# Gathers of a deformable convolution: how many leave at a time, and how far ahead of the matmuls

## The chip, the cores and the metric

The kernel runs on one core of one Trainium2 chip. The metric is device time of one execution in microseconds (us), the median of several runs. TensorE is called PE here, VectorE DVE, ScalarE ACT, GpSimd POOL and SyncE SP, as in the profile.

## The reference

The input x is 4 images of 64 channels and 32 x 32 pixels. Two layers follow each other, both with a residual:

```python
x = x + conv_ref(_ln_c(x), offset_w, offset_b, mask_w, mask_b, weight, bn...)
#   offset = conv3x3(x) + offset_b; mask = sigmoid(conv3x3(x))
#   for each pixel and each of 9 taps: 4 corners around a shifted position,
#   gathered from x, weighed bilinearly, times mask; einsum with weight; batch norm; silu
t = _to_tokens(x)
t = t + ffn_ref(_ln_t(t), sigma, phi, M_u, M_phi_plus, M_phi_minus, log_weights, gumbel)
#   causal convolution of all channels with 16 filters phi (and with alternating signs),
#   mixed by the matrices M_phi (weights of 4 branches of different length), plus 3 lags by M_u
```

## The kernel before

The pixels of two images (a pair, `bp` = 0 or 1) are processed together. A pair has 4 *quarters* of 256 tokens, so there are 8 quarters `q`. A quarter has 4 blocks `k` (2 pixel parities p x 2 images b2), each of 128 pixels x 9 taps. For each block and tap POOL issues one indirect DMA (`G<-corner_table,idx`, line 296): it fetches 128 rows of 1 KB, the four corners, from a table in DRAM, by the indices `idx`. That is 36 gathers a quarter, 288 in all, in the order of blocks and taps; `i` = 9k + tap counts them in their quarter. `G` has one slot for each block, so the gathers of a block also wait until the block of the quarter before has been weighed (`v_ready`).

DVE weighs a block when its nine gathers have landed (`weigh`, lines 490 to 494: three TENSOR_TENSOR, the last writes `V`). PE transposes V (`turn_values`, lines 905 and 906), ACT copies it to vT (line 696), PE convolves it with the weights (`convolve_values`, line 915), ACT copies y_chan (line 701), PE turns it back (`turn_convolved`, line 921), ACT takes the exponential (line 706, `expo`), and DVE does silu, residual and the second layer norm (`finish` = `activate` + `normalise`, lines 502 to 525), which ends with `u_ready`. `positions(q)` and `weights(q)` on DVE make the indices and corner weights of a quarter two ahead.

The second layer is 8 *passes* `n`, one per quarter. A pass has 16 steps (`convolve(i)`, lines 1017 to 1028: f16 matmuls into two PSUM banks by turns, 3(j+1) matmuls a step, j = n mod 4, so passes 3 and 7 are the longest and 0 and 4 the shortest). After each step ACT copies the bank to `u_conv` (line 739), and a later step waits for that copy. `conv_done[b2]` counts the steps: step i raises `conv_done[i % 2]`. Every fourth step PE mixes a group (`mix_group`, line 978), which ends with `group_mixed`; ACT's copy of `mixed` (line 744) waits for that after the last group of a pass. `HOSTED_AT` puts the PE work of the first layer for quarter n + 1 into pass n: `turn_values` at steps 5 and 12, `convolve_values` at 6 and 13, `turn_convolved` at 7 and 14. Between two passes lies a chain: exponential, `finish(q, 1)`, then the matmuls of `step_odd_tokens` (line 992).

Ahead of pass 0 stands the prologue: layer norm, the convolution for offsets and masks of both pairs (`convolve_offsets`, line 852, then `turn_offsets`, 862), normalised pixels turned (`turn_normalised`, 833; counted by `n_turned`), mixing matrices summed (882, `mats_summed`), filter rows made and stored (`f_rows_ready`), the second pair's pixels scaled on ACT (line 640, `n_ready`), the main weights turned (`w_turned`), the whole first layer for quarter 0 (`finish(0, 0)`, `finish(0, 1)`), then four scalings of the mixing matrices and two weighings of quarter 1 on DVE. The gathers of quarter 0 and most of quarter 1 lie in it.

All gathers leave in the order of one instruction stream. `keep_pace(q, i)`, called ahead of each gather, puts waits into POOL's stream that hold gather i of quarter q, and all behind it, until other engines have reached some point. In the passes the point is a step: it is linear in i, STEPS = 16 steps of convolution for BLK x TAPS = 36 gathers, `LEAD` gathers back.

Of the kernel before, what the change touches and what calls it, by code (L numbers as in the profile page):

```python
# [11 lines left out]
BP = B // 2  # L12
# [3 lines left out]
BLK = 4  # L16
TAPS = 9
# [9 lines left out]
STEPS = 4 * N_GROUPS  # L27
HALF = T // 2
BRANCHES = 4
# [3 lines left out]
START = 2  # L33
# [4 lines left out]
RSQRT_SEED = float(0x5F3759DF)  # L38
TAP_HALVES = (range(0, 5), range(5, 9))
WARM_UP = 4  # L40
LEAD = 22
WARM_AGAIN = 6


# [5 lines left out]
def metaformer_kernel(nc, x, offset_w, offset_b, mask_w, mask_b, weight, gamma, beta, mean, var,  # L50
                      sigma, phi, m_u, m_plus, m_minus, log_weights, gumbel, ident_in, grid_in, first_row_in, out):
    ctx = ExitStack()
    with ctx:
# [9 lines left out]
        def ap(a, offset, dims):  # L63
# [104 lines left out]
        x_turned, x_copied, n_ready, n_turned, n_copied = (  # L168
            sem(n) for n in ("x_turned", "x_copied", "n_ready", "n_turned", "n_copied"))
        woff_ready, woff_turned, woff_copied = sem("woff_ready"), sem("woff_turned"), sem("woff_copied")  # L170
        w_ready, w_turned, w_copied = sem("w_ready"), sem("w_turned"), sem("w_copied")
        phi_turned, f_rows_ready, f_rows_stored = sem("phi_turned"), sem("f_rows_ready"), sem("f_rows_stored")
        diag_ready, f_scale_ready, f_scale_done = sem("diag_ready"), sem("f_scale_ready"), sem("f_scale_done")
        w_diag_ready, mats_summed, mu_summed = sem("w_diag_ready"), sem("mats_summed"), sem("mu_summed")
        mats_ready, mu_ready, uT_zeroed = sem("mats_ready"), sem("mu_ready"), sem("uT_zeroed")
        off_done, off_laid, off_turned, off_copied, mask_exp = (
            sem(n) for n in ("off_done", "off_laid", "off_turned", "off_copied", "mask_exp"))
# [3 lines left out]
        v_ready = [sem(f"v_ready{i}") for i in range(2)]  # L181
        val_copied, y_done, y_exp, y_used, u_ready = (
            sem(n) for n in ("val_copied", "y_done", "y_exp", "y_used", "u_ready"))
        val_turned, y_convolved, y_copied = sem("val_turned"), sem("y_convolved"), sem("y_copied")
        u_turned, u_copied = sem("u_turned"), sem("u_copied")
        filt_loaded = [sem(f"filt_loaded{k}") for k in range(K)]
        conv_done = [sem(f"conv_done{i}") for i in range(2)]
# [75 lines left out]
        def _(pool):  # L263
# [4 lines left out]

            def keep_pace(q, i):

                step, last = (STEPS * (q - 1) + STEPS * (m - LEAD) // (BLK * TAPS) for m in (i, i - 1))
                if q >= 2 and (step != last or i == 0):
                    pool.wait_ge(conv_done[step % 2], step // 2 + 1)
                if q == 0 and i == TAPS:
                    pool.wait_ge(off_turned, 2)
                if q == 0 and i in (20, 25, 30):
                    pool.wait_ge(mats_summed, (i - 15) // 5 * 2 + 2)
                if q == 1 and i == 4:
                    pool.wait_ge(n_turned, 8)
                if q == 1 and i == 20:  # L280
                    pool.wait_ge(off_turned, 2 * BP)

            for bp in range(BP):
                for q in range(4 * bp, 4 * bp + 4):
# [838 lines left out]
```

## Time and profile before

| | us |
|---|---|
| median of 3 runs | 618.11 (615.82 to 621.09) |
| the profiled execution | 615.08 |
| its span, first to last instruction | 613.2 |
| PE busy | 466.6 (76% of the span), mean granted clock 0.852 |
| DVE busy | 308.9 (50%) |
| POOL busy | 291.0 (47%) |
| ACT busy | 226.2 (37%) |
| DMA moved | 53.95 MB, 88 GB/s on the mean |

The times in the rows are us from the start of the span unless marked ns. `x20` is a number of instructions put together in one row; the bracket at a row's end is how long the engine had been idle before it and what ended the idleness. "issue" there means that nothing the profile shows was waited for, "remote" that the releaser is unknown. The end of a PE instruction is modelled, not seen; the start of an ACT, DVE or POOL instruction is seen. The granted clock is a share of TensorE's full speed; its levels are 0.5 (1.2 GHz) and 1 (2.4 GHz).

### The profile page before, as it was taken

To read this page: it belongs to the slowest core of one execution; us is meant where nothing else is said; L and a number is where in the kernel's file an instruction comes from. 1 tells how busy PE (TensorE), PEld (TensorE's weight loads), DVE (VectorE), ACT (ScalarE), POOL (GpSimd) and SP (SyncE) were. 2 spreads that over 40 slices of the span, in tenths; PEclk is the share of its full clock that TensorE was granted. 3 is DMA by queue.
4 is the path that set the end of the run, shared out by engine and by line. 5 is a ranking of instruction groups with operands and counts; after the bars stand their busy time and mean duration, and the time that the engine had idled before them with its cause. 6 is when DMAs were issued, how large, how long until landed. Compare 5 with 4: busy or idle time off the path is not lost.

```text
span 613.2 us, 8001 instructions
## 1 busy us (share of the span) xinstructions
PE 466.6 (76%) x3022; PEld 256.5 (42%) x3022; DVE 308.9 (50%) x762; ACT 226.2 (37%) x515; POOL 291.0 (47%) x295
## 2 busy tenths in 40 slices
PE   4967559645666787699879996676678758998996
PEld 3522331422453444345435553444244424554543
DVE  5638752229996365637463746383636363612000
ACT  1126430015433453343434334433344334443432
POOL 1057747470374666466646664755476637000000
PEclk9877767558777898799989998877688969999999
DMA  7925933390132332233313321322133212100000
GB/s 156 177 78 166 339 103 103 96 342 18 36 91 64 87 90 83 64 92 94 86 55 95 87 85 55 100 78 77 56 92 95 86 48 92 33 1 1 10 0 10
DMA packets 43631, 53.95 MB, mean 88 GB/s; under 512 B 24536, under 2 KB 34014, under 8 KB 43593
## 3 DMA queue, kind: packets, MB, share of 16 engines
q0 software_dynamic: 13824, 37.77, 20.7%
q1 hardware_dynamic: 23745, 13.42, 8.5%
q10 hardware_dynamic: 6024, 2.26, 1.7%
q8 instruction: 24, 0.39, 0.3%
q14 instruction: 14, 0.11, 0.1%
HBM read 50.12 MB, written 3.30 MB: 87 GB/s over the span
## 4 chain that ended last, share of the span: by engine, by line
PE 49%; DVE 15%; issue 12%; another core or an unknown queue 10%; ACT 10%; DMA 2%; POOL 1%; SPq 1%; ACTq 0%; DVEq 0%
PE bank L1017 20%; PE bank L978 7%; ACT u_conv L739 6%; PE bank L852 5%; PE bank L1026 3%; PE bank L915 3%; PE bank L833 2%; PE bank L905 2%; DVE G L490 2%; DVE sil L503 2%; PE bank L882 1%; PE bank L862 1%; DMA filt<-in_L_ffn_phi_dram 1%; PE bank L824 1%
## 5 line engine op out<-in xcount | busy, mean ns | idle before, releaser
L296 POOL DMA_INDIRECT G<-corner_table,idx x288 | 288.4, 1001 | 231.4 <-issue 75.3
L1017 PE MATMUL bank<-filt,u 128*128 128x512 f16 (+1 forms) x960 | 206.9, 364 | 3.1 <-ACT u_conv L739 3.0
L739 ACT COPY u_conv<-bank 64x512 f32<-64x512 f32 x256 | 148.5, 580 | 160.4 <-PE bank L1017 60.7
L1017 PEld LDWEIGHTS bank<-filt,u 128*128 128x128 f16 x960 | 93.8, 102 | 104.4 <-issue 29.5
L490 DVE TENSOR_TENSOR G<-G,bank 128x2304 f32<-128x2304 f32 x32 | 81.6, 2551 | 73.2 <-DMA G<-corner_table,idx 71.4
L978 PE MATMUL bank<-u_conv,mixw 128*64 128x256 f32 (+1 forms) x640 | 71.1, 357 | 9.1 <-issue 8.8
L978 PEld LDWEIGHTS bank<-u_conv,mixw 128*64 128x64 f32 x640 | 43.1, 144 | 31.2 <-issue 21.4
L1026 PE MATMUL bank<-filt,u 64*128 64x256 f16 x168 | 30.0, 287 | 29.3 <-ACT u_conv L739 29.1
L494 DVE TENSOR_TENSOR V<-G 128x576 f32<-128x576 f32 x32 | 24.3, 758 | 41.3 <-PE bank L906 27.6
L491 DVE TENSOR_TENSOR G<-G 128x1152 f32<-128x1152 f32 x32 | 43.4, 1358 | 1.1
L502 DVE TENSOR_SCALAR expo<-expo 128x128 f32<-128x128 f32 x16 | 4.0, 250 | 70.1 <-ACT expo L706 51.8
L915 PE MATMUL bank<-vT,w_main 128*64 128x128 f32 (+1 forms) x320 | 27.7, 313 | 10.2 <-issue 6.8
L852 PE MATMUL bank<-filt,w_off 64*32 64x512 f32 x144 | 31.0, 688 | 4.3 <-issue 4.1
L905 PE MATMUL bank<-ident_swap,V 128*128 128x128 f32 x128 | 23.4, 320 | 10.6 <-DVE V L494 5.6
L1026 PEld LDWEIGHTS bank<-filt,u 64*128 64x128 f16 x168 | 11.9, 96 | 44.7 <-ACT u_conv L739 32.0
L1028 PE MATMUL bank<-filt,u_early 64*128 64x256 f16 x168 | 30.0, 287 | 0.0
L696 ACT COPY vT<-bank 128x512 f32<-128x512 f32 x32 | 17.2, 589 | 31.7 <-remote 16.2
L915 PEld LDWEIGHTS bank<-vT,w_main 128*64 128x64 f32 (+1 forms) x320 | 22.3, 158 | 15.0 <-issue 14.9
L905 PEld LDWEIGHTS bank<-ident_swap,V 128*128 128x128 f32 x128 | 18.0, 166 | 13.4 <-issue 13.1
L385 DVE TENSOR_TENSOR offs<-grid,bank 128x216 f32<-128x216 f32 x4 | 1.5, 380 | 34.5 <-PE bank L862 34.5
L761 ACT CAST u<-bank 128x256 f16<-128x256 f32 x8 | 3.0, 372 | 41.6 <-PE bank L994 33.6
L992 PE MATMUL bank<-u,ladder 128*128 128x256 f16 x8 | 2.7, 335 | 19.8 <-DVE u L525 19.8
(174 smaller groups left out, 425.6 us busy)
## 6 DMA issues: line engine op xcount, KB each, us to landing
filt<-filter_rows SPq DMA_DIRECT2D x16, 514.0 KB
G<-corner_table,idx POOLq DMA_INDIRECT x288
corner_table<-n_uT SPq DMA_DIRECT2D x12, 128.0 KB, 3.5
mixw<-in_x_dram SPq DMA_DIRECT2D x2, 512.0 KB, 6.2
filt<-in_L_ffn_M_phi_plus_dram SPq DMA_DIRECT2D x4, 256.0 KB
out_dram<-o_sb ACTq DMA_DIRECT2D x8, 128.0 KB, 2.2
filt<-n_L_ffn_M_phi_minus_dram ACTq DMA_DIRECT2D x2, 256.0 KB
corner_table<-n_uT ACTq DMA_DIRECT2D x4, 128.0 KB, 4.4
```

The lines of the kernel that those rows point to most:

```text
L296: pool.indirect_dma_start(G[:, k, tap, :], None, corners[bp], bass.IndirectOffsetOnAxis(ap=idx[:, q % 2, k, tap:tap + 1], axis=0)).then_in ...
L490: link(dve.tensor_tensor(g, g, w, ALU.mult))
L491: link(dve.tensor_tensor(G[:, k, :, 0:2 * C], G[:, k, :, 0:2 * C], G[:, k, :, 2 * C:4 * C], ALU.add))
L494: dve.tensor_tensor(V[:, b2].rearrange("s (t c) -> s t c", c=C), G[:, k, :, 0:C], G[:, k, :, C:2 * C], ALU.add).then_inc(v_ready[b2], 1)
L739: act.copy(u_conv[C * par:C * par + C, g % 2, :, b2, p, :], conv_ps[b2][rows].rearrange("c (k a) -> c k a", k=GROUP)).then_inc(conv_copied ...
L852: last = pe.matmul(bank[b2][group:group + NCH, :], w_off[half, tap, :], a, start=(t == 0), stop=(tap == TAP_HALVES[tg][-1]))
L905: pe.transpose(val_ps[b2][:, P * m:P * m + P], V[:, b2, P * m:P * m + P], ident)
L915: last = pe.matmul(y_chan_ps[C * b2:C * b2 + C, :], w_main[0:rows, m, :], vT[0:rows, b2, m, :], start=(m == 0), stop=(m == 4))
L978: last = pe.matmul(acc_ps[n % 2][C * p:C * p + C, 0:2 * P].rearrange("e (b a) -> e b a", b=2)[:, :, a0:a1], mixw[:, s, C * k:C * k + C], u ...
L1017: last = pe.matmul(out_of[b2][:, :, a0:P], u16[:, NJ * bp + j2, hl, b2, par:par + 2].rearrange("s w c -> s (w c)"), filt_h[:, ks, par, par ...
L1026: last = pe.matmul(out_of[0][:, :, 0:C], u16[C:P, n, hl, 0, par:par + 2].rearrange("s w c -> s (w c)"), filt_h[C:P, ks, par, part, 2:2 + C ...
L1028: pe.matmul(out_of[1][:, :, 0:C], u_early[:, hl, par:par + 2].rearrange("s w c -> s (w c)"), filt_h[0:C, ks, par, part, 2 + C:2 + P], star ...
```

## The change

Only the waits in POOL's stream change. In the passes (quarters 2 to 7) a wait stands before gathers 0 and 18 alone, and the step that it asks for is counted with LEAD = 14: step 9 of pass q-2 for gather 0, step 1 of pass q-1 for gather 18. Before, nearly every second or third gather had a wait, from step 6 of pass q-2 for gather 0 to step 5 of pass q-1 for gather 35. In quarters 0 and 1, before, six waits stood; after, quarter 0 has 11 and quarter 1 has 13, about one for every three gathers.

```diff
-LEAD = 22
+LEAD = 14
...
             def keep_pace(q, i):
 
-                step, last = (STEPS * (q - 1) + STEPS * (m - LEAD) // (BLK * TAPS) for m in (i, i - 1))
-                if q >= 2 and (step != last or i == 0):
+                step = STEPS * (q - 1) + STEPS * (i - LEAD) // (BLK * TAPS)
+                if q >= 2 and i % (2 * TAPS) == 0:
                     pool.wait_ge(conv_done[step % 2], step // 2 + 1)
-                if q == 0 and i == TAPS:
-                    pool.wait_ge(off_turned, 2)
-                if q == 0 and i in (20, 25, 30):
-                    pool.wait_ge(mats_summed, (i - 15) // 5 * 2 + 2)
-                if q == 1 and i == 4:
-                    pool.wait_ge(n_turned, 8)
-                if q == 1 and i == 20:
-                    pool.wait_ge(off_turned, 2 * BP)
+                if q == 0:
+                    if i == 3:
+                        pool.wait_ge(n_turned, 4)
+                    if i == 9:
+                        pool.wait_ge(off_turned, 2)
+                    if i == 11:
+                        pool.wait_ge(x_turned, 4)
+                    if i == 14:
+                        pool.wait_ge(mats_summed, 2)
+                    if i == 17:
+                        pool.wait_ge(f_rows_ready, 1)
+                    if i == 20:
+                        pool.wait_ge(v_ready[0], START + 1)
+                    if i == 23:
+                        pool.wait_ge(pixels_scaled, 1)
+                    if i == 26:
+                        pool.wait_ge(mats_summed, 2 * BRANCHES - 1)
+                    if i == 28:
+                        pool.wait_ge(v_ready[1], START + 1)
+                    if i == 30:
+                        pool.wait_ge(n_ready, 3)
+                    if i == 33:
+                        pool.wait_ge(w_turned, 1)
+                if q == 1:
+                    if i == 0:
+                        pool.wait_ge(n_turned, 8)
+                    if i == 3:
+                        pool.wait_ge(y_convolved, 1)
+                    if i == 7:
+                        pool.wait_ge(off_done, 3)
+                    if i == 10:
+                        pool.wait_ge(off_done, 4)
+                    if i == 13:
+                        pool.wait_ge(off_turned, 2 * BP)
+                    if i == 15:
+                        pool.wait_ge(v_ready[1], START + 2)
+                    if i == 17:
+                        pool.wait_ge(val_turned, START + 2)
+                    if i == 20:
+                        pool.wait_ge(y_convolved, 2)
+                    if i == 23:
+                        pool.wait_ge(u_ready, 2)
+                    if i >= 27 and i % 3 == 0:
+                        pool.wait_ge(conv_done[1], (i - 24) // 6 + 1)
```

## Rows read from the trace of the kernel before

**Rows 1.** The page's group of the gathers: busy us, mean ns of one, idle.
```profile
L296 POOL DMA_INDIRECT G<-corner_table,idx x288 | 288.4, 1001 | 231.4 <-issue 75.3
```

**Rows 2.** Stretches: length, busy (x) of PE, PEld, DVE, ACT, POOL, clock, DMA.
```profile
198.00:258.00 60.00, 44.81 (x315) 25.41 (x314) 33.64 (x78) 24.62 (x51) 36.12 (x36) 0.87 0.28 82
258.00:318.00 60.00, 52.04 (x347) 27.48 (x346) 33.10 (x78) 24.47 (x50) 35.28 (x36) 0.96 0.28 82
318.00:379.00 61.00, 56.71 (x382) 30.19 (x381) 33.20 (x78) 24.29 (x50) 36.59 (x36) 0.98 0.28 80
379.00:442.00 63.00, 42.09 (x309) 25.20 (x308) 33.48 (x78) 24.39 (x50) 35.81 (x36) 0.74 0.26 78
442.00:503.00 61.00, 43.08 (x313) 24.18 (x312) 30.07 (x61) 24.11 (x49) 37.38 (x36) 0.86 0.27 81
503.00:557.00 54.00, 48.72 (x346) 26.61 (x345) 24.31 (x57) 24.07 (x49) 13.80 (x14) 0.98 0.12 37
557.00:613.00 56.00, 51.57 (x336) 25.91 (x334) 0.00 (x0) 20.85 (x40) 0.00 (x0) 1.00 0.02 6
```

**Rows 3.** ACT's waits from 143 to 526 us: total, times, longest.
```profile
ACT u_conv L739 <- remote: 46.2, 14, 7.5
```

**Rows 4.** Timeline of PE in pass 1 (start, length, what, how many).
```profile
203.01 1.97 PE L978 MATMUL bank<-u_conv,mixw 128*64 128x128 f32 x32
```

**Rows 5.** Timeline of ACT in pass 1.
```profile
201.25 1.19 ACT L739 COPY u_conv<-bank 64x512 f32<-64x512 f32 x2 [1.23 <-PE bank L1017]
...
209.05 0.37 ACT L744 COPY mixed<-bank 128x256 f32<-128x256 f32 x1 [4.77 <-remote]
```

**Rows 6.** Timeline of POOL in pass 1, after its pause.
```profile
209.37 0.95 POOL L296 DMA_INDIRECT G<-corner_table,idx  x1 [1.63 <-remote]
```

**Rows 7.** Busy time by stretch, in the two longest runs with PE at work.
```profile
88.00:98.00 10.00, 9.20 (x61) 2.09 (x58) 6.92 (x16) 1.79 (x6) 7.68 (x8) 0.98 0.36 106
98.00:114.00 16.00, 12.16 (x17) 1.42 (x15) 0.00 (x0) 0.59 (x1) 10.42 (x11) 0.52 0.33 98
383.00:392.00 9.00, 7.38 (x70) 4.77 (x67) 3.91 (x2) 4.45 (x9) 6.86 (x8) 0.87 0.37 106
392.00:402.00 10.00, 4.79 (x27) 2.28 (x22) 2.76 (x2) 2.49 (x5) 6.77 (x7) 0.68 0.34 102
```

**Rows 8.** Timeline of POOL: one of the prologue, first and last of sixteen.
```profile
45.58 0.94 POOL L296 DMA_INDIRECT G<-corner_table,idx  x1 [4.51 <-DVE idx L406]
...
379.22 0.95 POOL L296 DMA_INDIRECT G<-corner_table,idx  x1 [3.87 <-PE bank L1017]
...
399.65 0.95 POOL L296 DMA_INDIRECT G<-corner_table,idx  x1 [0.30 <-issue]
```

**Rows 9.** Timeline of PE in the prologue.
```profile
31.25 5.06 PE L852 MATMUL bank<-filt,w_off 64*32 64x512 f32 x36
...
68.66 0.42 PE L906 MATMUL bank<-ident_swap,V 128*64 128x128 f32 x1
...
88.97 7.66 PE L852 MATMUL bank<-filt,w_off 64*32 64x512 f32 x53
...
113.19 1.01 PE L852 MATMUL bank<-filt,w_off 64*32 64x512 f32 x1 [1.08 <-issue]
...
124.63 2.40 PE L915 MATMUL bank<-vT,w_main 128*64 128x128 f32 x20 [1.51 <-ACT vT L697]
```

**Rows 10.** Timeline of ACT in the prologue, three copies of what PE made.
```profile
84.09 1.07 ACT L696 COPY vT<-bank 128x512 f32<-128x512 f32 x2 [12.12 <-remote]
...
106.85 0.59 ACT L665 COPY filt<-bank 128x512 f32<-128x512 f32 x1 [16.63 <-remote]
...
133.75 0.27 ACT L701 COPY y_chan<-bank 128x128 f32<-128x128 f32 x1 [9.27 <-remote]
```

**Rows 11.** Timeline of DVE in pass 1, a weighing and the end of the pass.
```profile
219.80 2.56 DVE L490 TENSOR_TENSOR G<-G,bank 128x2304 f32<-128x2304 f32 x1 [3.89 <-DMA G<-corner_table,idx]
...
249.81 0.23 DVE L502 TENSOR_SCALAR expo<-expo 128x128 f32<-128x128 f32 x1 [7.25 <-ACT expo L706]
```

## The prediction

> **What bounds the kernel now.** The page comes first: of its span of 613.2 us POOL is busy for less than half, and the gathers, which the change moves, are 288 instructions of POOL of 1.0 us each [rows 1]. The profiled execution took 615.08 us, 1.9 more than its span and 3.0 (0.5%) under the median of 618.11. The sum below is made against 615.1 and is not corrected for that half per cent.
>
> The busy time by stage comes next. The last stretch, 557 to 613 us, has the longest convolutions and no gather, and PE is idle there for 56.0 - 51.6 = 4.4 us; I take that as what a pass loses without gathers. Stretches with 36 gathers leave PE idle for 60 - 44.8 = 15.2, 60 - 52.0 = 8.0, 61 - 56.7 = 4.3, 63 - 42.1 = 20.9 and 61 - 43.1 = 17.9 us, and 503 to 557 for 5.3 [rows 2]. So PE sets the time of the passes, and something tied to the gathers takes PE time from the light ones. Those five and the sixth exceed 4.4 us by 10.8, 3.6, 0, 16.5, 13.5 and 0.9: 45.3 us. For pass 0 I add 3.7, as much as pass 2, and take 49 us.
>
> What takes it? ACT's waits name it badly: "remote", 46.2 us in 14 waits before the copies to u_conv [rows 3]. One of them can be followed. PE's mixing group starts at 203.01 and lasts 1.97 us [rows 4]. ACT, which needs only that for its copy of mixed, starts it at 209.05, 4.1 us after the recorded end, idle for 4.77 us [rows 5]. POOL had paused for a step of PE too, for 1.63 us, and went on at 209.37 [rows 6]. So PE's completions reached nobody for 4 us while a run of gathers drained. In a run a gather takes 0.95 us and the next starts 0.30 behind it [rows 8]. When a run goes on, PE itself starves: from 88 to 98 us PE starts 61 matmuls, from 98 to 114, under one run of gathers (8 and 11 of them in the two stretches), 17 matmuls in 16 us. In the passes the only long run, 16 gathers from 379.2 to 400.6 [rows 8], shows the same: 70 matmuls in its stretch from 383 to 392, then 27 in 10 us [rows 7]. I read this as: some 8 to 10 us into a run of gathers PE's results stop getting out, until the packets have drained. Today's pacing asks for a PE step every two or three gathers; when PE falls silent POOL must stop too, the run drains, and the stall ends after 3 to 4 us. The pacing is a loop that limits the damage.
>
> **The change, part by part.**
>
> Prologue, quarter 0. The waits at gathers 3, 9, 11, 14, 17, 20 and 23 are for things that are there by then (gather 9 starts at 45.58 [rows 8]); so 28 gathers still go nearly unbroken until weigh(0, 0, 1). What bites is gather 33, which waits for turn_weights. PE ends the transposes of V at 68.66 + 0.42 = 69.1, ACT gets them at 84.09 [rows 9, 10]. Gathers 9 to 32, 24 of them at 1.25 us, end 30 us after 45.6, and the pause before gather 33 lets the packets drain at about 78: gain 6 us on the path to convolve_values(0) and positions(1).
>
> Prologue, quarter 1. Twenty gathers in a run become groups of three or four. The 72 matmuls of convolve_offsets(1, ...) take 25 us (from 88.97 to 113.19 + 1.01) where 36 took 5.06 [rows 9], so about 11 for all with some at half clock: gain 13 us, as these groups follow off_done one by one. The convolution of the second values ends at 124.63 + 2.40 = 127.0 and its copy starts at 133.75, after 9.3 us idle [rows 9, 10]; a group of three does not hold it: 6.7 us. The waits added in quarter 1 hold only the gathers behind them on POOL; DVE needs the last two groups of them (values of the second half) only after scale_mixing and two weighings in pass 0. Sum of the prologue: 6 + 13 + 6.7, about -26 us. Bounds: 0, if groups merge into runs since their waits are long fulfilled; -38, the three remote waits of ACT whole (12.1 + 16.6 + 9.3) [rows 10].
>
> Passes. No instruction is added to or taken from any engine but POOL's waits: for each of quarters 2 to 7 some sixteen become two. Gathers 0 to 17 leave at once when step 9 of pass q-2 is done (before: from step 6 on, paced), gathers 18 to 35 when step 1 of pass q-1 is done (before: from step 14 of the pass before to step 5). So there are 12 runs of 18, each 17 x 1.25 + 0.95 = 22.2 us long [rows 8], with some 2 us of draining behind it, my estimate. Nothing inside a run depends on PE's steps, so the loop that ended a stall is gone. The stall lasts from about 9.4 us after the first gather to 24.2: 14.8 us. How much PE does in it is bounded by two rows: 17 matmuls in 16 us against 6.1 per us before (17% of its rate), and 27 in 10 us against 7.8 (35%) [rows 7]. That costs 14.8 x 0.83 = 12.3 or 14.8 x 0.65 = 9.6 us; I take 10.4, nearer to the run that was in a pass. Both rows also give bounds for a whole run: 27 instead of 78 is 6.6 us, 17 instead of 98 is 13.3 us.
>
> 12 x 10.4 = 125. Away go the 49 us that the short runs cost. The run that leaves at step 9 lasts over the pass boundary, where PE waits for DVE anyway, for no more than the 4.4 us [rows 2]: at most 6 x 4.4 = 26, I take half, 13. Passes: 125 - 49 - 13 = +63 us.
>
> DVE. The second half lands about 24 us after step 1 and not 18 (before, in pass 1: step 1 copied at 201.25 [rows 5], the last weighing at 219.8 [rows 11]). finish(q, 0) stands behind it on DVE and behind that the weighing of the next quarter; but DVE then stands idle 7.25 us before it gets the next expo [rows 11], and its work is needed only at steps 12 and 15. The 6 us disappear in that, all the more as PE is late too. If that cover were gone, 6 passes would lose 6 us each.
>
> Sum: 615.1 - 26 + 63 = 652 us.
>
> A rule speaks against all of this. The Trainium skill, SBUF — State Buffer, section "Who interferes with whom", says that DMA never contends with a compute engine and that PE never waits on anyone. By that rule the length of a run means nothing to PE and the sum would be 615 us. The trace does not agree as far as it goes: 17 matmuls in 16 us.
>
> **The rivals.**
>
> - A run costs PE a fixed toll, whatever its length. The 216 gathers of the passes leave today in runs of about 8, 27 of them, for 49 us: 1.8 us each on the mean, 4.1 for the one shown. Twelve long runs at these prices cost 22 to 49 us, and 615 - 26 - (27 to 0) = 562 to 589 us. It decides if a run of 18 costs less than (49 + 26) / 12 = 6.2 us, the point of no change. Against it: the two long runs seen.
> - The run's length costs nothing in the passes but the light ones: PE goes ahead in its queue, the boundary hides the rest. Passes within 10 us of before, the prologue wins: 590 to 605 us. For it: from 318 to 379 us PE loses nothing to 36 gathers [rows 2]. Against: these were short runs.
> - PE is not hurt by gathers at all (the rule above); what is read as starving has another cause that stays: 615 us, within 1%.
> - The prologue's small groups merge, as in quarter 0, and the gain there is nil, with the passes as forecast: 615 + 63 = 678 us, up to 700.
>
> **How the numbers follow.** Forecast (652 us; its own range 625 to 675): 0.5. Merged prologue, 678: 0.12. No effect: 0.1. Fixed toll: 0.16. Hidden in the passes: 0.12. One per cent is about what a measurement of this kernel can tell from no change. Slower: 0.5 + 0.12 - 0.01 = 0.61, as the low bound of the forecast (12 x 6.6 - 49 - 26 = +4) ends there; same 0.11; faster 0.28. The range 590 to 690 us leaves out most of the fixed toll and the ends.
>
> **What would show it.** Right: POOL's timeline has twelve unbroken runs of 18 from the second quarter on; in each, PE's matmuls per us fall to a third or less some 9 us in, with "issue" idle in the middle of L978 or L915 and ACT waits for "remote" of 5 to 15 us; the granted clock falls in these stretches; PE idle per light pass is above 25 us. In the prologue the first convolution of pass 0 starts near 117 us and not 143, and L852 ends its second 72 matmuls in about 12 us. Wrong: matmuls per us stay up through a run (then a fixed toll or none), or POOL's runs are cut by the v_ready waits into pieces of 9, or pass 0 starts later than 135 us. The forecast fails as a whole if a run of 18 costs PE less than 6.2 us.

## The result and the profile after

| | before | changed |
|---|---|---|
| median | 616.97 us (615.31 to 621.09, 4 runs) | 748.18 us (736.30 to 751.74, 4 runs) |
| ratio | | 1.2037, 95% interval 1.1946 to 1.2128 |
| profiled execution | 615.08 us, span 613.2, clock 0.74 to 1.00 in the passes [rows 2] | 736.30 us, span 734.3 |
| pass 0 begins (first copy to u_conv) | 144.3 us | 123.3 us |

The kernel is 20% slower: the prologue gained 21 us, the passes lost some 150. The medians are of all four runs and the ratio of the fast ones alone (736.30 and 745.77 us of the changed kernel), so it is a little under the quotient of the medians. The profiled execution of the changed kernel is 1.6% under its median; I say below which of the two a number goes by. Lines of kernel.py have moved by 36: L296 is L332 now, L739 is L775, L1017 is L1053, L852 is L888.

First the page: the chain that ended last by engine, then three groups (busy us, mean ns of one, idle us before them and what ended most of it).

```profile
PE 40%; another core or an unknown queue 32%; ACT 12%; DVE 8%; issue 7%; DMA 1%; SPq 0%; ACTq 0%; DVEq 0%
...
L332 POOL DMA_INDIRECT G<-corner_table,idx x288 | 280.5, 974 | 351.9 <-PE bank L1053 224.3
L775 ACT COPY u_conv<-bank 64x512 f32<-64x512 f32 x256 | 148.5, 580 | 319.2 <-remote 215.3
...
L526 DVE TENSOR_TENSOR G<-G,bank 128x2304 f32<-128x2304 f32 x32 | 81.6, 2550 | 129.0 <-DMA G<-corner_table,idx 128.9
```

The gathers themselves are as long as before [rows 1]. What has grown is the idle time of those who wait for PE: ACT's "remote" before the copies to u_conv was 46.2 us in 14 waits [rows 3]; now it is 215.3 us, and the chain is "another core or an unknown queue" for 32% (10% before). Busy time by stretch, a pass each (of the four left out three take 80 to 83 us, the one with 18 gathers 69):

```profile
123.00:192.00 69.00, 32.31 (x285) 20.93 (x284) 47.05 (x104) 23.94 (x48) 31.72 (x31) 0.72 0.21 60
192.00:277.00 85.00, 48.25 (x317) 26.78 (x316) 32.98 (x78) 24.52 (x51) 34.59 (x36) 0.76 0.19 58
...
360.00:447.00 87.00, 60.72 (x379) 31.68 (x378) 32.82 (x78) 23.93 (x49) 34.74 (x36) 0.82 0.19 56
...
679.00:734.00 55.00, 50.71 (x332) 25.53 (x330) 0.00 (x0) 20.03 (x37) 0.00 (x0) 1.00 0.02 6
```

The last stretch, which has no gather, is as before [rows 2]. All others are longer, and the heavy ones too: the pass that had lost nothing (61 us, 56.7 busy) now takes 87 us with 60.7 busy. PE's busy time grows as well, since its granted clock falls (0.98 to 0.82 there): in all twelve runs it is at the lower of its two levels when PE comes back.

POOL has twelve unbroken runs of 18, the first from 147.3 us, the last from 613.2. One of them in the timeline: ACT, then PE, then the first and the last gather of POOL.

```profile
405.69 1.19 ACT L775 COPY u_conv<-bank 64x512 f32<-64x512 f32 x2 [1.53 <-PE bank L1062]
425.13 1.18 ACT L775 COPY u_conv<-bank 64x512 f32<-64x512 f32 x2 [18.25 <-remote]
429.54 0.58 ACT L775 COPY u_conv<-bank 64x512 f32<-64x512 f32 x1 [3.23 <-remote]
...
409.33 4.75 PE L1053 MATMUL bank<-filt,u 128*128 128x512 f16 x24
426.37 0.39 PE L1062 MATMUL bank<-filt,u 64*128 64x256 f16 x1 [12.29 <-ACT u_conv L775]
...
403.71 0.95 POOL L332 DMA_INDIRECT G<-corner_table,idx  x1 [18.38 <-PE bank L1053]
...
425.32 0.94 POOL L332 DMA_INDIRECT G<-corner_table,idx  x1 [0.30 <-issue]
```

PE ends its 24 matmuls at 414.08. ACT, which copies from the bank that they fill, is told at 425.13, 11 us later and as POOL issues its last gather; PE then starts again, having waited 12.3 us for that copy. By its record PE is not slow here, its word, the semaphore by which it tells the others, is not passed on (the end is modelled, so I cannot tell a late end of the last matmul from a late word). What PE still did in the run was work for which banks were free.

I call such a stretch a hold. It is not complete. In ten of the twelve runs single results still get out later than 6 us into it, nearly all of them late. In the run from 232.78 us one does so in the middle, and ACT's own word reaches PE at once, 0.6 us after the first of its two copies:

```profile
245.66 1.18 ACT L775 COPY u_conv<-bank 64x512 f32<-64x512 f32 x2 [10.64 <-remote]
...
246.89 0.39 PE L1062 MATMUL bank<-filt,u 64*128 64x256 f16 x1 [7.27 <-ACT u_conv L775]
```

Nor does the hold end with the last gather: in all twelve runs ACT starts on one of PE's results 25.5 to 25.9 us after the first gather, 4 us after the last is issued (21.6) and 1.5 to 2 us after its last packet (23.9 to 24.2).

One long run in the same trace holds nothing. The last 13 gathers of quarter 1 leave in pass 0, and ACT starts as PE's last transposition ends, 16 us into that run (POOL, PE, ACT):

```profile
122.13 1.69 POOL L332 DMA_INDIRECT G<-corner_table,idx  x1 [4.52 <-DVE u L561]
...
139.83 0.95 POOL L332 DMA_INDIRECT G<-corner_table,idx  x1 [0.30 <-issue]
...
137.94 0.42 PE L942 MATMUL bank<-ident_swap,V 128*64 128x128 f32 x1
...
138.40 1.07 ACT L732 COPY vT<-bank 128x512 f32<-128x512 f32 x2 [6.33 <-PE bank L942]
```

Three of its gathers take 1.7 to 2.0 us in place of 0.95. Whether that is what spares PE was not tried.

### The profile page after: what moved, and what is told of

Read it like the earlier page. It is cut to its first block, busy times and chain, and to the rows that moved or that the text cites. A ratio compares the mean times of both kernels' runs of the same rounds, so it can differ in the third digit from the quotient of the medians.

```text
span 734.3 us, 7991 instructions
## 1 busy us (share of the span) xinstructions
PE 465.1 (63%) x3022; PEld 258.0 (35%) x3022; DVE 308.6 (42%) x762; ACT 226.9 (31%) x515; POOL 283.2 (39%) x295
## 3 DMA queue, kind: packets, MB, share of 16 engines
q0 software_dynamic: 13824, 37.77, 17.2%
## 4 chain that ended last, share of the span: by engine, by line
PE 40%; another core or an unknown queue 32%; ACT 12%; DVE 8%; issue 7%; DMA 1%; SPq 0%; ACTq 0%; DVEq 0%
PE bank L1053 16%; ACT u_conv L775 7%; PE bank L1014 7%; PE bank L1062 3%; PE bank L951 3%; PE bank L888 3%; PE bank L941 1%; PE bank L918 1%; DVE sil L539 1%; DMA filt<-in_L_ffn_phi_dram 1%; ACT vT L732 1%; ACT filt L669 1%; ACT n_uT L676 1%; DVE G L526 1%
## 5 line engine op out<-in xcount | busy, mean ns | idle before, releaser
L332 POOL DMA_INDIRECT G<-corner_table,idx x288 | 280.5, 974 | 351.9 <-PE bank L1053 224.3
L775 ACT COPY u_conv<-bank 64x512 f32<-64x512 f32 x256 | 148.5, 580 | 319.2 <-remote 215.3
L1053 PE MATMUL bank<-filt,u 128*128 128x512 f16 (+1 forms) x960 | 212.2, 369 | 37.9 <-issue 23.1
L1053 PEld LDWEIGHTS bank<-filt,u 128*128 128x128 f16 x960 | 94.5, 103 | 145.4 <-issue 59.1
L526 DVE TENSOR_TENSOR G<-G,bank 128x2304 f32<-128x2304 f32 x32 | 81.6, 2550 | 129.0 <-DMA G<-corner_table,idx 128.9
L1062 PE MATMUL bank<-filt,u 64*128 64x256 f16 x168 | 33.4, 313 | 111.2 <-ACT u_conv L775 105.3
L1014 PE MATMUL bank<-u_conv,mixw 128*64 128x256 f32 (+1 forms) x640 | 77.0, 375 | 17.2 <-issue 17.2
L1062 PEld LDWEIGHTS bank<-filt,u 64*128 64x128 f16 x168 | 12.7, 102 | 128.9 <-ACT u_conv L775 111.6
L951 PE MATMUL bank<-vT,w_main 128*64 128x128 f32 (+1 forms) x320 | 25.8, 312 | 23.0 <-ACT vT L733 21.5
L941 PE MATMUL bank<-ident_swap,V 128*128 128x128 f32 x128 | 27.7, 361 | 13.8 <-issue 7.2
L538 DVE TENSOR_SCALAR expo<-expo 128x128 f32<-128x128 f32 x16 | 3.6, 227 | 75.3 <-ACT expo L742 75.1
L1064 PE MATMUL bank<-filt,u_early 64*128 64x256 f16 x168 | 33.5, 314 | 0.0
L941 PEld LDWEIGHTS bank<-ident_swap,V 128*128 128x128 f32 x128 | 21.1, 190 | 17.8 <-issue 17.2
L732 ACT COPY vT<-bank 128x512 f32<-128x512 f32 x32 | 17.1, 584 | 26.7 <-remote 11.3
L888 PE MATMUL bank<-filt,w_off 64*32 64x512 f32 x144 | 21.0, 765 | 0.0
L918 PE MATMUL bank<-filt,u_conv 128*128 128x512 f32 x16 | 11.3, 846 | 9.2 <-ACT x_tok L661 4.7
L539 DVE RECIPROCAL sil<-expo 128x128 f32<-128x128 f32 x16 | 15.3, 953 | 0.5
```

Source lines behind the costliest of these rows:

```text
L332: pool.indirect_dma_start(G[:, k, tap, :], None, corners[bp], bass.IndirectOffsetOnAxis(ap=idx[:, q % 2, k, tap:tap + 1], axis=0)).then_in ...
L526: link(dve.tensor_tensor(g, g, w, ALU.mult))
L732: act.copy(vT[:, b2, 0:4, :], val_ps[b2][:].rearrange("k (m s) -> k m s", m=4))
L775: act.copy(u_conv[C * par:C * par + C, g % 2, :, b2, p, :], conv_ps[b2][rows].rearrange("c (k a) -> c k a", k=GROUP)).then_inc(conv_copied ...
L888: last = pe.matmul(bank[b2][group:group + NCH, :], w_off[half, tap, :], a, start=(t == 0), stop=(tap == TAP_HALVES[tg][-1]))
L941: pe.transpose(val_ps[b2][:, P * m:P * m + P], V[:, b2, P * m:P * m + P], ident)
```

## The experiments

**Which edit does it.** Two kernels with one half of the change each, and two that go from one to the other. In all of them but e1 the rest is the changed kernel. The kernel before was timed again beside each experiment, and its medians were 608 to 622 us; so two experiments from different groups are compared by their ratios to it, and some ten us between their times show nothing.

e1 is the kernel before with the changed passes only:

```diff
-LEAD = 22
+LEAD = 14
...
-                if q >= 2 and (step != last or i == 0):
+                if q >= 2 and i % (2 * TAPS) == 0:
```

> The kernel before with only the passes changed: 12 runs of 18 gathers, LEAD 14; the waits of quarters 0 and 1 as before. The theory of the run's length (PE's results stay in while a run of gathers goes on, from about 5 us into it until its packets are drained) puts the whole loss here: the trace of the changed kernel has pass 0 start 20 us earlier than before (123.3 against 143), so this one should come out 20 us above the changed kernel, at 765 to 772 us. If the many waits of the prologue cost something in the passes, it comes out below 748.

Measured: 750.64 us (745.79 to 752.75), ratio 1.2245 (1.2146 to 1.2343) to the 614.21 of before. That is less than I expected (765 to 772 us): by the ratios the new prologue saves 13 us with the long runs behind it, and not 20. The loss is all in the passes, and ACT's "remote" is there without the new prologue:

```profile
ACT u_conv L739 <- remote: 193.6, 22, 23.1
```

e2 is the other half: the changed prologue, the wait at each step, LEAD = 22.

> The changed kernel with the passes of before (a wait for every step, LEAD 22). By the same theory the prologue's gain stands alone: 617 - 20 = 597 us, with pass 0 starting near 123 us. If the prologue's waits only shift the work into pass 0, it comes out at 612 to 622.

Measured: 591.21 us (589.64 to 594.03), ratio 0.965 (0.9583 to 0.9718), so the prologue gives 21.5 us, and pass 0 begins at 123.2 us. It beats both kernels.

e3 is e2 with LEAD = 14, so that it has all of the change but the runs:

> The changed kernel with LEAD 14 kept, but a wait for every step as before: the lead alone. Length theory: no run is longer than POOL's pauses allow, so within 10 us of the kernel with the prologue alone, 595 to 607 us. Rival, the later release: gathers that come 3 to 4 steps later make DVE late, PE waits for V at steps 5 and 12, and most of the loss stands without any long run: over 680 us.

Measured: 609.06 us (605.45 to 613.53, 10 runs), ratio 0.994 (0.9894 to 0.9986). The lead alone costs 18 us. The waits of DVE for gathers show where (e3, then e2):

```profile
DVE G L526 <- DMA G<-corner_table,idx: 180.1, 27, 13.0
```

```profile
DVE G L526 <- DMA G<-corner_table,idx: 74.2, 17, 6.4
```

e8 is the changed kernel with LEAD = 22:

> The changed kernel (runs of 18) with the step of the wait 22 gathers back as before, instead of 14. It parts the two edits of the passes. If they add up: e3 against e2 gave 18 us for the 8 gathers of lead, so 748 - 18 = 730 us (720 to 740). If the lead costs only where gathers leave by twos and threes, since a run of 18 holds PE wherever it stands: 740 to 755 us. If the place of a run within the pass decides (a run from step 6 and one from step 14 in place of steps 9 and 1): below 700 us.

Measured: 691.2 us (687.1 to 692.62), ratio 1.1318 (1.1265 to 1.1371). My sum (730) was wrong and so was the second theory; the time is where I had put it if the place of a run decides (below 700). With runs of 18 the lead is worth 57 us by the times, 44 by the ratios. Its waits of DVE and ACT:

```profile
DVE V L530 <- PE bank L942: 174.3, 12, 20.4
...
DVE G L526 <- DMA G<-corner_table,idx: 7.1, 5, 2.1
```

```profile
ACT u_conv L775 <- remote: 110.9, 14, 16.0
```

DVE no longer waits for gathers (7.1 us against 128.9) but for PE's transpositions, and ACT's "remote" is half. The runs now begin at steps 6 and 14 of the passes, so one of each pair lies over the boundary between passes; the first has joined the gathers of quarter 1 into a run of 31. That this place is why a hold costs less there is my reading of it; no run moved the place alone.

**How the length of a run matters.** The wait every 9 gathers instead of 18 (e4; every 6 in e5; every 6 and every 4 in e10 and e11, these with LEAD = 22):

```diff
-                if q >= 2 and i % (2 * TAPS) == 0:
+                if q >= 2 and i % TAPS == 0:
```

> The changed kernel with a wait before every ninth gather of quarters 2 to 7 (24 runs of 9, 11 us each plus draining), LEAD 14. Length theory with a linear law, stall = run - 5 us: 24 x (13 - 5) = 192 us against 12 x (24 - 5) = 228, so 36 us less than 748: 712 us; if the stall of one run is worked off in the pause behind it, as in the kernel before with its runs of 7 to 9, some 620 to 640. Rival, a fixed toll per run: twice as many runs, so over 850 us.

> The changed kernel with a wait before every sixth gather, lead 14: 36 runs of 6 in place of 12 of 18. 6 gathers are in flight for 6 x 1.24 = 7.4 us. If the hold starts about 4 us into a flight and lasts to its end: 36 x 3.4 = 122 us over what no hold at all gives (530 by m1): 640 to 660 us, no better than the runs of 9 (24 x (10.7 - 4) = 161, found 656 - 530 = 126). If PE, released for a moment, works off what is queued, short holds cost less than their length: 605 to 630 us, between e3 (609) and e4 (656).

> A candidate for the best kernel: the changed prologue, runs of 6, lead 22. Runs of 6 cost no more than twos and threes at lead 14 (603 against 609). The lead of 22 gave 18 us at twos and threes and 57 us at eighteen. If it gives the same here: 575 to 590 us, faster than the 591 of e2. If the gathers, at 1.24 us each and 45 us a quarter, fill a pass of 50 us whatever their grouping, and runs of 6 join into flights of 14 us: 590 to 600 us.

> The same with runs of 4 (5.0 us in flight each, just past the 4 us at which the holds began in the profile). If short holds are what is left in e2 (its flights are 8 to 11 us, two or three of its steps joined): 575 to 588 us. If joins happen all the same, since POOL has only some 5 us to spare in a pass: 588 to 597 us.

| gathers between waits | unbroken runs | LEAD | us | ratio (95%) | ACT's "remote" before u_conv, us (times) |
|---|---|---|---|---|---|
| 18 (changed) | 18 | 14 | 748.2 | 1.204 (1.195 to 1.213) | 215.3 (23) |
| 9 (e4) | 9, one of 18 | 14 | 656.5 | 1.072 (1.063 to 1.082) | 99.0 (23) |
| 6 (e5) | 18 of 6, 9 of 12 | 14 | 602.9 | 0.989 (0.983 to 0.995) | 45.6 (9) |
| 2 to 3 (e3) | 1 to 9, one of 14 | 14 | 609.1 | 0.994 (0.989 to 0.999) | 24.7 (7) |
| 18 (e8) | 18, one of 31 | 22 | 691.2 | 1.132 (1.127 to 1.137) | 110.9 (14) |
| 6 (e10) | 23 of 6, 6 of 12 | 22 | 577.6, and 592.6 to 593.9 three times | no interval | 8.4 (4) |
| 4 (e11) | 16 of 4, 15 of 8, 12, 16 | 22 | 602.6 | 0.988 (0.980 to 0.996) | 34.2 (11) |
| 2 to 3 (e2) | 2 to 9, one of 16 | 22 | 591.2 | 0.965 (0.958 to 0.972) | 34.6 (12) |

The runs are read from POOL's timeline in the passes. A wait that is already fulfilled cuts nothing, so e5, e10 and e11 have runs of twice their number and more.

From 18 to 9 at LEAD 14 the time falls by 92 us (81 by the ratios), from 9 to 6 by 54 (51). Against m7 below, which has no holds, a run of 18 costs 15.5 us and one of 9 costs 94 / 24 = 3.9: twice the length, four times the price. So neither a fixed toll for each run nor a price for each gather fits, but a hold that begins some way into a run does. For e4 both of my numbers missed: 656 stands between 712 (losses in proportion to the length) and 620 to 640 (short holds worked off). e5 came out 2 us below the lower of my two ranges.

With LEAD = 22 fewer gathers between waits gave nothing that is shown. e11 missed both of its ranges on the high side; its runs of 8 and more say that it did not try runs of 4. For e10 575 to 590 came in one execution of four, so whether it is faster than e2 stays open.

e9 is e2 with LEAD = 26:

> The changed kernel's prologue, the passes with a wait at each step as before, but the step 26 gathers back instead of 22. Going from 14 to 22 gave 18 us (e3, e2), by gathers that are through before DVE asks for them. If that goes on: 591 - 5 to 9 = 582 to 586 us. If at 22 the gathers are early enough already and what is left is the hold by flights of 8 to 11 us: 588 to 594 us. If buffers not yet free (POOL waits for V of the quarter before) bunch them into longer runs: 600 us and more.

Measured: 590.88 us (589.44 to 594.27), ratio 0.9709 (0.9662 to 0.9757), where e2 has 0.965: a longer lead gives nothing more.

**What holds PE's word back.** Four kernels change what leaves in the runs of 18, with the changed kernel's waits. In m1 and m2 the gathers of quarters 2 to 7 are plain transfers of 128 rows of 1 KB from fixed places, issued by POOL (m1) or by SP (m2), so that these quarters are computed from other pixels:

```diff
+                            if q >= 2:
+                                pool.dma_start(G[:, k, tap, :], ap(table[bp], (k % 2 * IMAGE + tap) * 2 * C, [[2 * C, P], [1, ROW]])
+                                               ).then_inc(gathered[k], 16)
+                                continue
                             pool.indirect_dma_start(
```

> The changed kernel; in quarters 2 to 7 each gather is a plain DMA from POOL instead: the same 128 rows of 1 KB into the same place, at fixed rows of the table, under the same waits (so those quarters compute from wrong pixels). If PE is held by the indirect form, the stalls go and the passes take their 55 us each: about 600 us. If it is held by the transfers that POOL's DMAs make, whatever their form, 730 to 750 us with the same gaps of ACT and PE.

> As the plain DMAs, but issued from SP in quarters 2 to 7, under the same waits at gathers 0 and 18 (those quarters compute from wrong pixels). If what holds PE is POOL at work (its descriptors), nothing holds PE now: 590 to 610 us. If it is the bytes that land in SBUF or the packets on the DMA engines, the stalls stay: over 700 us, or fewer but denser ones, since SP issues a DMA in 0.4 us and not in 1.25.

Measured: 530.28 us (ratio 0.8526, 0.8478 to 0.8575) and 527.54 us (0.8482, 0.8433 to 0.8531), 60 us and more below what I expected without stalls, and what the short runs of the kernel before cost would be gone too. A run of m1 on POOL, and then most of what ACT waits for before u_conv:

```profile
246.80 9.50 POOL L333 DMA_DIRECT2D G<-corner_table  x18 [12.59 <-PE bank L1057]
```

```profile
ACT u_conv L779 <- PE bank L1057: 81.0, 51, 5.0
ACT u_conv L779 <- PE bank L1066: 53.2, 52, 2.5
```

"Remote" is there before u_conv once, for 2.4 us. The plain transfers take the same queue as the gathers (q0, software_dynamic) with as many packets (13824) and bytes (37.77 MB), so neither the queue nor the traffic is what holds PE. The bytes of 18 gathers leave in 9.5 us; e4's runs of 9 indirect gathers are of about that length (8 x 1.25 + 0.95 = 11 us) and have 99.0 us of "remote".

m3 fetches 256 bytes of each row instead of 1 KB, m5 fetches for 64 partitions instead of 128 (each leaves the rest of G stale in quarters 2 to 7):

```diff
-                                G[:, k, tap, :], None, corners[bp],
+                                G[:, k, tap, 0:ROW if q < 2 else C], None, corners[bp],
```

> The changed kernel; in quarters 2 to 7 a gather fetches 256 B of each row and not 1 KB (three corners are left out, so those quarters compute from stale data). Instructions and rows stay, bytes fall to a quarter. If the bytes in flight hold PE: stalls mostly gone, about 600 to 640 us. If POOL's work or the number of descriptors holds it: 730 to 750 us as before.

> The changed kernel; from quarter 2 on every gather fetches rows for 64 partitions instead of 128, with as many instructions, waits and the same length of row (the upper half of G keeps what quarters 0 and 1 left, so that quarters 2 to 7 are computed from wrong pixels). It asks what the length of the hold on PE hangs on. If on the rows that POOL's queue works through: a run of 18 is in flight for about half of its 22.3 us and costs what a run of 9 cost in e4 (656 - 597 over 24 runs, some 3 to 7 us each): 600 to 650 us. If on the number of gather instructions, whatever each fetches: the flights stay at 22 us and the time at 735 to 755 us. With 256-byte rows (m3) nothing changed, so bytes are out already.

Measured: 747.7 us (ratio 1.2022, 1.1875 to 1.217) and 742.47 us (1.2182, 1.2129 to 1.2235). The groups of the gathers, m3 and then m5:

```profile
L332 POOL DMA_INDIRECT G<-corner_table,idx x288 | 279.7, 971 | 360.1 <-PE bank L1053 236.1
```

```profile
L333 POOL DMA_INDIRECT G<-corner_table,idx x288 | 271.4, 942 | 366.0 <-PE bank L1054 238.2
```

Neither a quarter of the bytes nor half of the rows shortens a gather on POOL or moves the time. The hold goes by the number of gather instructions in a row, or by the time that they take; these two I could not part, since a gather takes about 0.95 us whatever it fetches.

m4 leaves out two of the three f16 products, so that PE has far fewer matmuls to announce:

```diff
-        products = ((0, 0), (0, 1), (1, 0))
+        products = ((0, 0),)
```

> The changed kernel with one of the three f16 products of each convolution (two correction products are left out). PE has a third of these matmuls; ACT's copies, the hosted work and the mixing stay. If PE is let do a certain number of instructions in a run before it is held (a queue that fills), the hold comes later in a run and a run of 18 costs less: below 560 us. If the hold is a matter of time since the run began, PE still stands for some 16 us in each of the 12 runs: 620 us or more, with the passes at about 70 us.

Measured: 666.33 us (663.35 to 669.3). ACT's waits:

```profile
ACT u_conv L775 <- remote: 107.3, 13, 23.1
```

Had the hold been a number of results that PE can put out, a third of them would have ended it (below 560 us). The time fell by 82 us, no more than PE's busy time did (465.1 to 376.6 us), and the longest "remote" is 23.1 us as in the changed kernel (23.0). Its sum before u_conv is half, but another 70.8 us of "remote" stand before ACT's copies to o_sb and 45.2 before vT, where the changed kernel has none and 11.3: the whole is about as much as in the changed kernel. The run speaks for a hold by time.

m7 has no transfer: two small memsets on POOL and a semaphore for DVE stand for each gather of quarters 2 to 7 (computed from what G holds).

> The changed kernel with each gather of quarters 2 to 7 replaced by two small memsets on POOL (about 1.1 us together) and a semaphore for DVE; same waits, same runs of 18, no transfer at all (quarters 2 to 7 are computed from what G holds of quarters 0 and 1). If POOL being busy, or its writes to the memory, is what holds PE: near 748 us. If it takes the gathers' own work, as the plain DMAs of m1 (530 us) suggest: 520 to 540 us.

Measured: 562.1 us (560.66 to 563.53), ratio 0.9235 (0.9146 to 0.9324). DVE's waits:

```profile
DVE G L545 <- POOLq L346: 105.0, 12, 11.5
```

So POOL may be busy for 42 us a quarter without holding PE. The time is over my 520 to 540 and 32 us (44 by the ratios) over m1. DVE waits longer for its input than in m1 (105.0 us against 54.7), since POOL delivers at 1.2 us apiece; that this is the whole difference is not shown. And m7 is the changed kernel without its holds: 748.2 - 562.1 = 186 us for 12 runs, 15.5 us each (by the profiled executions 736.3 - 560.7 = 176, 14.6 each; by the ratios, 1.2037 - 0.9235 of some 615 us, 172, 14.4 each).

**What ends a hold.** m6 leaves the waits as they are and puts four small memsets (2.5 us) behind every third gather:

```diff
                             ).then_inc(gathered[k], 16)
+                            if q >= 2 and tap % 3 == 2:
+                                for _ in range(4):
+                                    fill()
```

`fill` is one memset of a spare tile of 128 x 576 that nothing else uses.

> The changed kernel, with four small memsets of a spare tile on POOL (about 2.2 us together) behind every third gather of quarters 2 to 7: the runs of 18 wait for PE as rarely as before, but 2 us without a gather stand after every 3.7 us of gathers. If the hold on PE begins some 4 us into an unbroken flight and ends when the flight does, each piece stays below it, and the losses go although POOL is slower by 12 x 2.2 = 26 us a quarter: between 530 (no hold at all) and about 650, where POOL itself (22.4 + 6 x 2.2 = 36 us for a run, 72 a quarter) would set the length of a pass. If what matters is that 18 gathers leave in one go without hearing from PE, gaps do not help, and the run only gets longer: 750 us or more.

Measured: 679.05 us (678.99 to 679.11), ratio 1.1157 (1.1055 to 1.1259). POOL in one run, DVE's and ACT's waits, and the chain that ended last:

```profile
378.59 0.95 POOL L342 DMA_INDIRECT G<-corner_table,idx  x1 [0.16 <-issue]
...
381.10 0.95 POOL L342 DMA_INDIRECT G<-corner_table,idx  x1 [0.30 <-issue]
382.05 2.50 POOL L277 MEMSET spare<- 128x576 f32 x4
384.70 0.95 POOL L342 DMA_INDIRECT G<-corner_table,idx  x1 [0.16 <-issue]
```

```profile
DVE G L539 <- DMA G<-corner_table,idx: 236.6, 26, 14.3
...
ACT u_conv L788 <- PE bank L1066: 77.2, 50, 5.0
```

```profile
POOL 59%; PE 17%; issue 14%; DVE 6%; DMA 2%; SPq 0%; ACT 0%; POOLq 0%
```

The "remote" before u_conv is down to 0.4 us although POOL asks PE no more often than in the changed kernel. POOL takes 36 x 1.25 + 12 x 2.65 = 77 us a quarter now, DVE waits for it, and by the chain POOL sets most of the 679 us. So it is the unbroken row of gathers that holds PE, and POOL needs no wait on PE to avoid it, only a pause.

Two kernels look for the shortest pause, both with LEAD = 22 (two memsets behind every fourth gather; one behind every third):

> The changed kernel (two waits a quarter) with lead 22 and two of the small memsets (some 1.2 us) behind every fourth gather of quarters 2 to 7, so that no more than 4 gathers (5 us) leave without a gap. POOL then takes 36 x 1.24 + 9 x 1.2 = 55 us a quarter against the 72 of m6. If a gap of 1.2 us ends a hold as the 2.3 us of m6 did, POOL sets the pass: 123 + 7 x 56 + 48 = 563, with the boundaries 560 to 580 us, faster than e2 (591). If so short a gap is not felt by the packets in flight, the runs count as 18 long and cost what e8 did: 680 to 720 us. If it ends most holds: 580 to 610.

> The same with one memset (some 0.6 us) behind every third gather: POOL takes 36 x 1.24 + 12 x 0.6 = 52 us a quarter. If a gap of any length will do: 545 to 570 us. If the gap has to outlast something like the 1.7 us between an issue and the end of its packets, 0.6 us is too short: 680 to 720 us, as e8 (691). Together with e12 and m6 this brackets the gap that ends a hold: 0.6, 1.2 or 2.3 us.

Measured: e12 569.95 us (569.89 to 572.25), ratio 0.9262 (0.919 to 0.9334), within my 560 to 580 and the fastest kernel of this study that computes everything; e13 611.3 us (605.46 to 615.74), ratio 0.9889 (0.979 to 0.9988), much better than e8 and far from e12, between my two ranges. ACT's "remote" before u_conv in e13:

```profile
ACT u_conv L787 <- remote: 51.0, 11, 10.7
```

e12 on POOL, ACT's waits for "remote" before u_conv, and two passes, the light one and the heaviest:

```profile
324.63 0.99 POOL L342 DMA_INDIRECT G<-corner_table,idx  x1 [0.30 <-issue]
...
327.18 1.00 POOL L342 DMA_INDIRECT G<-corner_table,idx  x1 [0.30 <-issue]
328.18 1.23 POOL L277 MEMSET spare<- 128x576 f32 x2
```

```profile
ACT u_conv L788 <- remote: 7.7, 1, 7.7
```

```profile
185.00:233.00 48.00, 39.53 (x314) 22.71 (x312) 33.22 (x78) 23.72 (x48) 39.50 (x45) 0.96 0.30 85
...
289.00:353.00 64.00, 57.69 (x383) 30.34 (x382) 36.82 (x78) 24.85 (x51) 52.60 (x61) 0.95 0.29 85
```

A pause of 1.2 us behind four gathers (5 us) ends nearly all holds (7.7 us of "remote" are left before u_conv, 17.8 before y_chan), one of 0.6 us behind three ends about half: e8's 110.9 us of "remote" are 51.0 here. The pass of 60 us with 44.8 busy [rows 2] takes 48 with 39.5; the heaviest, which had lost nothing, takes 64 for 61.

## Why the prediction was wrong in size

It said 652 us (590 to 690) by this sum: 615 - 26 in the prologue - 49 that the short runs cost + 12 runs of 10.4 - 13 hidden at the boundaries. Direction and mechanism were right: twelve runs of 18, PE starved within them, the loop of small waits that had limited the damage. The time was 96 us more than that. Term by term:

**The price of a run (10.4) is the step that failed.** I had "from about 9.4 us after the first gather to 24.2: 14.8 us", at 35% to 17% of PE's rate. The runs show a stretch that begins at 6 us and ends at about 26, and 14.4 to 15.5 us lost. Busy time in the changed kernel from 6 to 26 us after the first gather of two of the twelve runs and the sum over all twelve, then the same of m7:

```profile
238.80:258.80 20.00, 5.89 (x28) 3.39 (x25) 4.24 (x3) 1.62 (x3) 12.53 (x13) 0.68 0.30 92
...
368.80:388.80 20.00, 11.11 (x55) 5.13 (x52) 4.05 (x3) 2.64 (x5) 12.58 (x13) 0.75 0.32 92
...
sum 240.00, PE 77.10 PEld 40.49 DVE 56.90 ACT 27.21 POOL 151.32; mean PE 6.42 PEld 3.37 DVE 4.74 ACT 2.27 POOL 12.61
```

```profile
205.90:225.90 20.00, 12.35 (x81) 7.58 (x81) 18.42 (x57) 5.62 (x12) 15.48 (x27) 0.83 0.00 1
...
294.40:314.40 20.00, 20.00 (x148) 11.29 (x147) 8.29 (x5) 9.30 (x19) 15.32 (x27) 1.00 0.02 7
...
sum 240.00, PE 192.27 PEld 118.12 DVE 155.32 ACT 108.84 POOL 195.25; mean PE 16.02 PEld 9.84 DVE 12.94 ACT 9.07 POOL 16.27
```

Over the twelve stretches PE starts 415 matmuls where m7's PE starts 1594: 26% (7% to 37% in the single runs; by busy time 40%, with part of it at the lower clock). The rate that I took (30%) was about right. The length was not: 20 us and not 14.8. 20 x (1 - 0.26) = 14.8 us a run, close to the 14.4 to 15.5 that m7 gives. Counted by 2 us from the first gather, over all twelve runs, the changed kernel's PE starts 187, 226, 138, 82, 74, 62, 52, 29, 16, 5, 11, 29, 40 and 116 matmuls, m7's 148, 188, 106, 141, 164, 188, 186, 223, 182, 188, 123, 105, 76 and 58: the two part at 6 us and meet again at 26. I had read the onset from runs that PE could bridge with work whose banks were free, and where I saw PE starve its results had been held for 3 us or so; and I had let the stall end with the packets, where the word came 1.5 to 2 us later. That is 12 x 4.4 = 53 of the 96 us.

**The boundaries (-13) gave nothing that can be seen**: the price by m7 is already net of whatever they hide, and it is not below 14.4. The remaining 8 us (12 x 0.7) are the difference between 14.8 and 15.5, a remainder and not a finding.

**The lead was costed at nothing, and costs 18 us** (e3 against e2). The cover that I named, 7.25 us of idle DVE, was not enough: DVE's waits for gathers rise from 74.2 to 180.1 us. I did price the loss of the cover ("6 passes would lose 6 us each", 36 us), and it came half.

**The prologue gave 21.5 us and not 26.** With the lead that is about what m7, which has no holds, shows beyond my 615 - 26 - 49 = 540 us: 562 - 540 = 22. The small groups of the prologue merged in part, since many waits were fulfilled when POOL reached them: the runs there are of 5, 16, 6, 10, 10, 3 and 13 gathers after the first nine, where they were of 27, 20 and 16. (Quarter 1 has 12 waits after the change, not 13.) The rows of the changed kernel that answer [rows 9, 10]:

```profile
75.14 1.04 ACT L732 COPY vT<-bank 128x512 f32<-128x512 f32 x2
...
99.35 0.59 ACT L701 COPY filt<-bank 128x512 f32<-128x512 f32 x1 [5.35 <-remote]
...
113.93 0.27 ACT L737 COPY y_chan<-bank 128x128 f32<-128x128 f32 x1 [6.04 <-remote]
```

PE, then the first and the last of ten gathers on POOL:

```profile
84.88 10.89 PE L888 MATMUL bank<-filt,w_off 64*32 64x512 f32 x72
...
99.58 0.95 POOL L332 DMA_INDIRECT G<-corner_table,idx  x1 [2.40 <-remote]
...
110.85 0.94 POOL L332 DMA_INDIRECT G<-corner_table,idx  x1 [0.30 <-issue]
```

Quarter 0: the copy of V comes at 75.1 and not 84.1, 9 us earlier where I said 6, of which 4 reach the next step (84.88 for 88.97). The 72 matmuls take 10.9 us, as forecast (12, from 25). The last copy of the prologue still has 6.04 us of "remote", since no group of three stands there but ten gathers in a row, and the word comes 3 us after the last is issued: of the 6.7 us I gave it only 3.2 came. Pass 0 starts at 123.3, forecast "near 117".

Together: 53 (price) + 8 + 13 (boundaries) + 18 (lead) + 4.5 (prologue) = 96.5. The close fit proves little, as 562 + 12 x 15.5 is 748 by the way the price was got; what was measured apart is the 20 us at 26%, the 18 of the lead and the 21.5 of the prologue.

**The rivals.** A fixed toll per run is excluded by e4 and e5, and the point of no change, 6.2 us a run, was passed by far. "Hidden in the passes" is excluded by the pass from 360 to 447 us, which takes 26 us more where short runs cost it nothing. Merged groups in the prologue came in part and took 4.5 us of the gain and not all of it. That gathers leave PE alone is the rival that needs two answers. For plain transfers it holds: in m1 and m2 18 of them in a row leave no trace on PE (530 and 528 us). For indirect gathers issued by POOL it does not. The Trainium skill, SBUF — State Buffer, section "Who interferes with whom", has DMA contend with no compute engine; m1 and m2 agree with it, and 415 matmuls for 1594 under the indirect runs do not. It does not go by the bytes, since m3's quarter of them changes nothing; what holds PE's word back the runs do not show.

## What to carry to other kernels

A long unbroken row of indirect gathers on POOL keeps most of PE's results from ACT, DVE and POOL: cut it into groups of at most four or so with a pause of more than a microsecond, by small work on POOL if there is none to wait for, rather than by waits on the engine that is being held. Then look at POOL's timeline, since waits that are already fulfilled cut nothing. When ACT or DVE waits long for something that PE has ended by its own records, look at what POOL is issuing, and measure where PE's word stops, not where PE runs dry, since work on free banks hides the first microseconds. And when a step is moved back, count the lead it loses by itself: here it was 18 us with the pacing that was there and 44 to 57 with long runs.

## What was not expected of the hardware

- In a run of 18 indirect gathers few of PE's results get out, nearly all late, until 25.5 to 25.9 us after the first gather (4 us after the last is issued), twelve times out of twelve; PE starts 26% of the usual matmuls from 6 to 26 us. ACT's word reaches PE within it after 0.6 us. A row of plain transfers from the same engine on the same queue does nothing of the kind.
- The hold does not depend on bytes (256 for 1024 a row: 747.7 us), rows (64 for 128: 742.5 us), or POOL's being busy (m7: 562.1 us). Whether it goes by gathers or by their time is open, and 13 gathers from 122.1 us, three of them of 1.7 to 2.0 us, held nothing.
- A gather mostly takes POOL 0.94 to 1.0 us whatever it fetches, a plain transfer of the same 128 KB 0.53 us (9.50 for 18).
- 1.2 us without a gather after each four ends the holds but for 7.7 us before u_conv, 0.6 us after each three only some of them.
